# Language adapter with residual and layer norm on one core: the beginning ordered anew, a constant lag of the second product, and the inverse deviation as a power on GpSimd

## What is computed

```python
w1 = W1[language_ids]; w2 = W2[language_ids]
h = jnp.einsum('bsh,bha->bsa', hidden_states, w1) + b1[language_ids][:, None, :]
h = jax.nn.relu(h)
adapted = jnp.einsum('bsa,bah->bsh', h, w2) + b2[language_ids][:, None, :]
x = hidden_states + adapted
mean = jnp.mean(x, axis=-1, keepdims=True)
var = jnp.mean(jnp.square(x - mean), axis=-1, keepdims=True)
normed = (x - mean) * jax.lax.rsqrt(var + LN_EPS)
return hidden_states + normed * gamma[language_ids][:, None, :] + beta[language_ids][:, None, :]
```

## Time and profile before

| | |
|---|---|
| median of 3 runs | 348.10 us (347.31 to 348.62) |
| the profiled execution | 348.07 us |
| its span (first to last instruction) | 346.3 us |
| TensorE, busy | 305.1 us, 88% |
| VectorE, busy | 313.9 us, 91% |
| ScalarE, busy | 238.5 us, 69% |
| GpSimd, busy | 172.7 us, 50% |

### The profile page before, as it was taken

How to read it: one execution, slowest core, us unless ns; L and a number is a source line. 1 busy time by engine, 2 the same in 40 slices (tenths; PEclk the granted TensorE clock), 3 DMA queues, 4 the chain that set the end, 5 groups by cost and what they waited for, 6 DMA issues and landing times. The chain is left out here.

```text
span 346.3 us, 8118 instructions
## 1 busy us (share of the span) xinstructions
PE 305.1 (88%) x2196; PEld 273.1 (79%) x2196; DVE 313.9 (91%) x690; ACT 238.5 (69%) x599; POOL 172.7 (50%) x207
## 2 busy tenths in 40 slices
PE   2597799999799999979999998999999688988843
PEld 1186799998799999879999996999999577878731
DVE  4849789999999999999999999999999978788783
ACT  4348767788677777767777786777778565756532
POOL 1000066665655555565555566666666654635440
PEclk9999999999999999999999999999999999999996
DMA  7999805777776777677677777676777762231313
GB/s 218 314 413 398 313 13 173 243 245 244 241 243 232 231 238 241 224 252 236 235 237 235 232 235 250 234 237 236 242 245 242 242 223 101 107 120 65 122 61 121
DMA packets 41678, 75.63 MB, mean 218 GB/s; under 512 B 2250, under 2 KB 7401, under 8 KB 41509
## 3 DMA queue, kind: packets, MB, share of 16 engines
q1 hardware_dynamic: 41538, 74.98, 63.8%
q10 hardware_dynamic: 99, 0.14, 0.1%
HBM read 41.56 MB, written 33.55 MB: 217 GB/s over the span
## 5 line engine op out<-in xcount | busy, mean ns | idle before, releaser
L266 POOL TENSOR_TENSOR x_io<-x_io,beta_all 128x512 f32<-128x512 f32 x128 | 161.5, 1283 | 0.2 <-issue 0.2
L360 PE MATMUL ps_h<-w_all,x_T 128*128 x1024 | 143.8, 284 | 0.0
L360 PEld LDWEIGHTS ps_h<-w_all,x_T 128*128 128x128 f32 x1024 | 126.1, 194 | 1.5
L318 ACT ACTIVATE cut<-ps_y,row_sum 128x512 bf16<-128x512 f32 x128 | 87.9, 687 | 37.7 <-PE ps_y L382 37.7
L503 DVE SCALAR_TENSOR_TENSOR ps_y<-ps_y,mean,gamma_all 128x512 f32<-128x512 f32 x128 | 90.7, 752 | 14.1 <-ACT cut L318 13.6
L263 POOL TENSOR_TENSOR mean<-row_sum,over_h 128x2 f32<-128x2 f32 x64 | 12.6, 196 | 161.8 <-DVE ps_y L494 161.8
L516 DVE SCALAR_TENSOR_TENSOR x_io<-ps_y,rstd,x_io 128x512 f32<-128x512 f32 x128 | 90.2, 746 | 2.6 <-POOL x_io L266 0.3
L296 ACT COPY x_T<-ps_T 128x512 f32<-128x512 f32 x128 | 74.9, 588 | 21.0 <-PE ps_T L352 20.7
L494 DVE SCALAR_TENSOR_TENSOR ps_y<-x_io,b_all 128x512 f32<-128x512 f32 x128 | 87.4, 723 | 1.7 <-issue 1.7
L352 PE MATMUL ps_T<-identity,x_io 128*128 128x128 f32 x512 | 78.5, 277 | 6.2 <-DMA x_io<-in_x 6.2
L382 PE MATMUL ps_y<-w_high,h_high 128*128 x128 | 56.3, 439 | 15.2 <-DVE h_low L483 15.1
(11 more groups left out here) (43 smaller groups left out, 163.6 us busy)
## 6 DMA issues: line engine op xcount, KB each, us to landing
x_io<-in_x SPq DMA_DIRECT2D x64, 512.0 KB, 4.4
out<-x_io SPq DMA_DIRECT2D x63, 512.0 KB, 3.0
w_all<-in_L_cond_W SPq DMA_DIRECT2D x5, 512.0 KB, 8.1
x_io<-in_L_cond_W SPq DMA_DIRECT2D x5, 512.0 KB, 8.8
b_all<-in_L_cond_b SPq DMA_DIRECT2D x1, 2560.0 KB, 16.3
out<-x_io SPq DMA_DIRECT2D x2, 256.0 KB, 2.1
x_io<-in_L_cond_gamma ACTq DMA_DIRECT2D x1, 60.0 KB
x_io<-in_L_cond_beta ACTq DMA_DIRECT2D x1, 60.0 KB
```

What stands on the lines that cost most here:

```text
L266: nc.gpsimd.tensor_tensor(x_slot(t), x_slot(t), of_lang(beta_all, langs[b]), ALU.add)\
L318: nc.scalar.activation(squares[:, t % 2, :], ps_y[t % Y_BANKS][:, :], ACT.Square, scale=-float(H), bias=stat(row_sum, t), accum_out=stat(s ...
L360: last = nc.tensor.matmul(part, x_T[:, t % 4, c, :], w1_all[:, bass.ds(lang, 1), c, :].rearrange("p o a -> p (o a)"), start=False, stop=(c ...
```

## The change

**Order.** `FIRST` is 4 and the catch-ups are gone: steps 4 to 63 each have one second product, four pairs behind the first, and the last four pairs' second products follow step 63. h has six buffers in place of seven. In TensorE's step, `turn_h(p - 1)` now stands behind the first transpose of x and ahead of the first product, so that h is turned one step later than it was. ScalarE's step is: copy of x, rounding of h of the step before, copy of x, copy of h, then the squares.

**Beginning.** All 20 spreads stand ahead of step 0, over six banks (the four `ps_y`, `ps_h` and `ps_hT`); ScalarE copies gamma and the odd rows of beta, VectorE the even rows of beta. TensorE waits for all copies ahead of step 0. gamma's load is issued by SyncE ahead of x; ScalarE's table load comes ahead of its two DMAs. ScalarE's high halves of W2 stand ahead of the steps 0, 1, 2 and (two chunks) 3, each with its wait for the mean.

**Inverse.** VectorE's reciprocal is gone. GpSimd raises the deviation to the power -1, of pair n - 1, between the mean of pair n and its two additions of beta.

```diff
-H_PAIRS = 7
-FIRST = 5
-CATCH_UP = (12, 25, 38, 51)
+H_PAIRS = 6
+FIRST = 4
...
+    SPREAD_BANKS = Y_BANKS + 2
+    by_act = [n for n in range(2 * L) if n < L or n % 2 == 1]
+    by_dve = [n for n in range(2 * L) if n not in by_act]
...
             sp.dma_start(ids_raw[:, :], ids.rearrange("(a b) -> a b", a=1)).then_inc(s_ids, 16)
+            sp.dma_start(x_io[0:3 * L, 2 * ROWS_PAIR, :],
+                         gamma.unsqueeze(0).broadcast_to([3, L, H])).then_inc(s_gamma_rows, 16)
             load_x(0)
...
+            def invert_pair(n):
+                pool.wait_ge(std_ready, n + 1)
+                nc.gpsimd.tensor_tensor(stats(rstd, n), stats(std, n), minus_one[:, 0:2], ALU.pow).then_inc(rstd_ready, 1)
 
             def add_beta(n):
                 langs = langs_of(pool, n)
                 pool.wait_ge(seeded, 2 * n + 2)
                 pool.wait_ge(x_turned, 2 * n + 2)
                 nc.gpsimd.tensor_tensor(stats(mean, n), stats(row_sum, n), over_h[:, 0:2], ALU.mult).then_inc(mean_ready, 1)
+                if n > 0:
+                    invert_pair(n - 1)
                 for b in range(2):
                     t = 2 * n + b
                     nc.gpsimd.tensor_tensor(x_slot(t), x_slot(t), of_lang(beta_all, langs[b]), ALU.add)\
                         .then_inc(x_beta_ready, 1)
 
             pool.wait_ge(ids_ready, 1)
-            pool.wait_ge(over_h_ready, 2)
-            for p in range(PAIRS):
-                for n in second[p]:
-                    if n == 0:
-                        pool.wait_ge(spread_act, L)
-                        pool.wait_ge(spread_dve, L)
-                    add_beta(n)
-            for n in rest:
+            pool.wait_ge(over_h_ready, 3)
+            pool.wait_ge(spread_act, len(by_act))
+            pool.wait_ge(spread_dve, len(by_dve))
+            for n in range(PAIRS):
                 add_beta(n)
+            invert_pair(PAIRS - 1)
 
...
-            thrice = "(g l) h -> g l h"
-            act.dma_start(x_io[0:3 * L, 2 * ROWS_PAIR, :],
-                          gamma.unsqueeze(0).broadcast_to([3, L, H])).then_inc(s_gamma_rows, 16)
+            act.wait_ge(set_ready, 4)
+            nc.scalar.activation(table_load[:, :], eps[:, :], ACT.Sqrt, bias=eps[:, 0:1])
             act.dma_start(b1_rows[:, :],
                           b1.unsqueeze(0).broadcast_to([3, L, A])).then_inc(s_b1_rows, 16)
             act.dma_start(x_io[0:3 * L, 2 * ROWS_PAIR + 1, :],
                           beta.unsqueeze(0).broadcast_to([3, L, H])).then_inc(s_beta_rows, 16)
-            act.wait_ge(set_ready, 4)
-            nc.scalar.activation(table_load[:, :], eps[:, :], ACT.Sqrt, bias=eps[:, 0:1])
...
+            def step(p):
+
                 if p < PAIRS - 1:
                     copy_x(2 * p + 2)
+                if p > 0:
+                    high_h(p - 1)
+                if p < PAIRS - 1:
                     copy_x(2 * p + 3)
                 copy_h(p)
-                for n in second[p]:
-                    square_pair(n)
-                split_h(p)
-                for n in w2_after[p]:
-                    high_w2(n)
-            for n in rest:
+
+            copy_x(0)
+            copy_x(1)
+            for n in by_act:
+                act.wait_ge(spread, n + 1)
+                nc.scalar.copy(spread_to(n), spread_bank(n)).then_inc(spread_act, 1)
+            high_w2(0)
+            step(0)
+            high_w2(1)
+            step(1)
+            high_w2(2)
+            step(2)
+            high_w2(3)
+            high_w2(4)
+            step(3)
+            for p in range(FIRST, PAIRS):
+                step(p)
+                square_pair(p - FIRST)
+            high_h(PAIRS - 1)
+            for n in range(PAIRS - FIRST, PAIRS):
                 square_pair(n)
 
...
             langs = {0: langs_of(pe, 0)}
+            pe.wait_ge(b1_parts_ready, 1)
+            pe.wait_ge(spread_act, len(by_act))
+            pe.wait_ge(spread_dve, len(by_dve))
+            pe.wait_ge(s_w1, 16 * W_CHUNKS)
             for p in range(PAIRS):
-                for n in spread_before[p]:
-                    spread_row(n)
-                if p == 0:
-                    pe.wait_ge(b1_parts_ready, 1)
-                    pe.wait_ge(s_w1, 16 * W_CHUNKS)
                 for b in range(2):
                     pe.wait_ge(x_T_ready, 2 * p + b + 1)
                     if p < PAIRS - 1:
                         turn_x(2 * p + 2 + b)
+                    if b == 0 and p > 0:
+                        turn_h(p - 1)
                     first_product(2 * p + b, langs[p][b])
                 if p < PAIRS - 1:
                     langs[p + 1] = langs_of(pe, p + 1)
-                for n in second[p][:1]:
-                    if n == 0:
-                        pe.wait_ge(w2_low_ready, L)
+                if p == FIRST:
+                    pe.wait_ge(w2_low_ready, L)
+                if p >= FIRST:
+                    n = p - FIRST
                     for b in range(2):
                         second_product(2 * n + b, langs[n][b])
-                turn_h(p)
-                for n in second[p][1:]:
-                    for b in range(2):
-                        second_product(2 * n + b, langs[n][b])
-            for n in rest:
+            turn_h(PAIRS - 1)
+            for n in range(PAIRS - FIRST, PAIRS):
                 for b in range(2):
                     second_product(2 * n + b, langs[n][b])
 
...
-            copy_spreads(0)
-            dve.wait_ge(over_h_ready, 2)
+            for n in by_dve:
+                dve.wait_ge(spread, n + 1)
+                nc.vector.tensor_copy(spread_to(n), spread_bank(n)).then_inc(spread_dve, 1)
+            dve.wait_ge(over_h_ready, 3)
             mean_of_w2(0)
             mean_of_w2(1)
+            low_w2(0)
+            mean_of_w2(2)
+            low_w2(1)
+            mean_of_w2(3)
             low_h(0)
-            low_w2(0)
-            copy_spreads(1)
-            low_w2(1)
-            mean_of_w2(2)
-            mean_of_w2(3)
+            low_w2(2)
+            mean_of_w2(4)
+            low_w2(3)
             low_h(1)
-            low_w2(2)
-            copy_spreads(2)
-            mean_of_w2(4)
+            dve.wait_ge(ids_ready, 1)
+            langs = {n: langs_of(dve, n) for n in range(2)}
+            low_w2(4)
+            dve.wait_ge(s_b2, 16)
+            seed_pair(0, langs[0])
             low_h(2)
-            low_w2(3)
-            copy_spreads(3)
-            low_w2(4)
+            dve.wait_ge(spread_act, len(by_act))
+            dve.wait_ge(spread_dve, len(by_dve))
+            seed_pair(1, langs[1])
             low_h(3)
-            dve.wait_ge(ids_ready, 1)
-            dve.wait_ge(s_b2, 16)
-            dve.wait_ge(spread_act, L)
-            dve.wait_ge(spread_dve, L)
-            langs = {n: langs_of(dve, n) for n in range(2)}
-            seed_pair(0, langs[0])
-            low_h(FIRST - 1)
-            seed_pair(1, langs[1])
 
...
-                invert_pair(n)
                 finish_pair(n)
...
-            for p in range(PAIRS):
-                for n in second[p]:
-                    norm_and_seed(n, p if n == second[p][0] else None)
-            for n in rest:
-                norm_and_seed(n, None)
+            for n in range(PAIRS):
+                norm_and_seed(n, n + FIRST if n + FIRST < PAIRS else None)
```

More of the change, by code:

```diff
@@ L34, in build @@
     out_pairs = out.rearrange("(n b) s h -> s n b h", b=2)
[L38 to L53, removed]
+    SPREAD_BANKS = Y_BANKS + 2
+    by_act = [n for n in range(2 * L) if n < L or n % 2 == 1]
+    by_dve = [n for n in range(2 * L) if n not in by_act]
+    assert FIRST + 2 <= H_PAIRS
     with ExitStack() as ctx:
@@ L196, in of_lang, with spread_bank, pair_of @@
             return table[:, bass.ds(lang, 1), :].rearrange("p o h -> p (o h)")
+        spread_banks = ps_y + [ps_h, ps_hT]
+        assert len(spread_banks) == SPREAD_BANKS
+        def spread_bank(n):
+            return spread_banks[n % SPREAD_BANKS][:, :]
+        def pair_of(bank):
+            return bank[:, 0:2 * S]
         def flat(pair_tile):
@@ L370, in turn_h @@
                 for b in range(2):
-                    last = nc.tensor.transpose(ps_hT[:, b * S:(b + 1) * S], h_rows[:, p % 2, b, :], identity[:, :])
+                    last = nc.tensor.transpose(pair_of(ps_hT)[:, b * S:(b + 1) * S], h_rows[:, p % 2, b, :],
+                                               identity[:, :])
                 last.then_inc(h_turned, 1)
@@ L388, in _ @@
             turn_x(1)
[L389 to L393 removed]
+            pe.wait_ge(pick_ready, 1)
+            pe.wait_ge(parts_zero, 2)
+            pe.wait_ge(gamma_parts_ready, 1)
+            for n in range(2 * L):
                 if n == L:
                     pe.wait_ge(beta_parts_ready, 1)
[L396 to L397 removed]
+                gone = n - SPREAD_BANKS
+                if gone in by_act:
+                    pe.wait_ge(spread_act, by_act.index(gone) + 1)
```

(8 more changed lines are left out.)

36 lines of the change are left out of this document (6 added, 30 removed).

## The result

| | us |
|---|---|
| before, median of 8 runs | 347.98 (347.26 to 348.62) |
| after, median of 8 runs | 345.6 (344.91 to 346.83) |
| ratio after / before | 0.994, 95% interval 0.992 to 0.996 |
| forecast | 331 (326 to 344) |
| profiled execution of after, its span | 344.8, granted clock 0.974 (before 346.3, 0.991) |

The account below looks back on a forecast made before the run. It took TensorE as the early bound, then VectorE, then engines waiting in turn. Step 5 at 42.8 us plus 264.0 of steps, a tail to 326.4, 2.64 to the span's end and 1.8 outside gave 331 us (326 to 344).

Parts of the forecast that it names:

- Part 1, constant lag: Without catch-ups, TensorE paces at 4.49 us per step and the slow last twelve pairs go, returning about 11 us.
- period of 5.44: Distance in us between scalings after the last catch-up, pairs 52 to 63, engines waiting in turn; forecast to vanish.
- Part 2, the power: Inverse on GpSimd between mean and additions: VectorE's work falls to 4.23 us per pair, and the power costs nothing mid-kernel.
- The ring: GpSimd and VectorE, every pair: end of mean, P, additions, seeds; 4.14 + P us, the bound if P exceeds 0.35.
- P: Length of GpSimd's 128x2 power, without a row in the trace: taken as 0.30 us, ends 0.15 and 1.26.
- Each waits for the other to end: VectorE's seeds and GpSimd's additions of beta lock each other out for whole instructions, so a held seeding takes 1.25 us.
- Part 3, the beginning: Loads 0.7 us later, x pair 4 landing at 34.7, step 5 starting at 42.8; the start worth 4.7 us.
- The sum: Whole kernel: TensorE leaves the steps at 306.8 us, the last four pairs follow, span 329.0, plus 1.8 outside: 330.8.
- rival 1: GpSimd and VectorE: the ring becomes the bound mildly, P from 0.35 to 0.6; 340 us at P = 0.5; chance 0.25.
- rival 2: GpSimd and VectorE: the ring makes the kernel slower than before, P > 0.63; 358 us at P = 0.8; chance 0.14.
- Rival 4: VectorE's seeds aren't held by GpSimd's additions, the tail runs at VectorE's pace, P hardly counts: 329.5 us; chance 0.10.
- Rival 3: The new beginning gives nothing, step 5 starting at 47.4 us: 335.5 us in all; chance 0.06.

Follow-up runs that it names:

- the product: The changed kernel with a product in place of the power on GpSimd, same place and operands: 333.4 us, ratio 0.960.
- the two powers: The changed kernel with the power taken twice, the first time into a spare tile: 387.6 us, ratio 1.115.
- the seed with one SBUF operand: The changed kernel with the seed's second input taken from the PSUM bank in place of b2: 332.3 us, ratio 0.955.
- x pair 4 early: The changed kernel with the load of x pair 4 issued ahead of b2's: 344.3 us, ratio 0.992.
- the reciprocal kernel: The changed kernel with the inverse back on VectorE as a reciprocal, nothing else undone: 332.3 us, ratio 0.957.
- its like with the power ahead of the mean: The changed kernel with the power ahead of the mean and x pair 4's load ahead of b2's, no catch-ups: 330.8 us, ratio 0.954.
- the kernel with the lowest median: The changed kernel with the reciprocal back on VectorE and x pair 4's load ahead of b2's: 329.4 us, ratio 0.947.

## Why the prediction was wrong, point by point

**Part 1, constant lag: right.** TensorE paces at 4.49 us wherever nothing is held, with 755 matmuls in 100 us, and no period of 5.44 is left. The kernel with this part alone gains 12.6 us. The forecast had put about 11 us here.

**Part 2, the power: right mechanism, wrong size.** The ring (end of the mean, P, additions, seeds) and its place are borne out by the product, the two powers and the seed with one SBUF operand. The term that failed is P: I took 0.30 us because a 128x2 product on the same engine took 0.15 to 0.20, and the power takes 0.67. Both ends, 0.15 and 1.26, held it; my choice between them rested on the number of columns, as if the operation were nothing. It was a number without a row and with a threshold right beside it, and the expected cost as a mean over its bounds would have been far from zero. From there the step "TensorE paces the middle and the power costs nothing there" was wrong: the ring paces, at 4.69 us.

The ring's other terms were too long by 0.12 us: measured they add up to 4.02, not 4.14, which moves the threshold from 0.35 to 0.47. The recorded formula with P = 0.67 gives a round of 4.81 and, by 61 (P - 0.35), a span near 349; measured are 4.69 and 344.8. The 0.12 lie in the hold. A seed takes 0.61 us to its accumulator's reading (152.97 to 153.58 above). In after's round the held seed ends at 157.78, so by that length it was running from 157.17 on, 0.13 us before the recorded end of the additions at 157.30. "Each waits for the other to end" overstated the hold by that much.

The three kernels without the power's cost (reciprocal, product, seed with one SBUF operand) take 332.3 to 333.4 us, where the forecast had 331 with a power that costs nothing. So the rest of the sum was short by 1 to 2 us only.

**Part 3, the beginning: the loads right, 2 us missed.** x pair 4 landed at 34.13 (forecast 34.7). From there I let step 3 take 3.1 us; it took 5.97, at a granted clock of 0.50 up to 38 us. These 2.9 us were put at nothing: the forecast had the wait for x, but not the lower clock behind it, where eight matmuls take 2.02 and 1.94 us in place of 1.11 and four transposes 1.09 and 1.06 in place of 0.60. Step 4 took 4.74 us where I had 5.0. Step 5 came at 44.84, not at 42.8. VectorE's halves of W2 were ready by 34.8, earlier than the 36.8 of the forecast, and TensorE shows no wait for them. That "x pair 4 early" gave a step 5 at 42.21, near the 42.5 written for it, is luck: TensorE waited for h_low in step 3 and ran at the lower clock after it, and neither was in the sum. Also, the starts were worth less than they read: the reciprocal kernel has step 5 at 43.53, the kernel with the lag alone has the like point, with pair 0's second product behind it, at 47.27, 3.7 us apart; the spans of these two executions are 3.3 apart and the medians 2.5.

**The sum.** Forecast span 329.0, measured 344.8. Step 5: +2.0. From there to the end of the seeds of pair 63: 278.4 us forecast, 336.49 - 44.84 = 291.65 measured, +13.3 (61 rounds at 0.20 more are 12.2, the first round of 5.20 us another 0.7). The tail behind these seeds: 7.8 forecast, 8.3 measured, +0.5. Together 15.8, the whole of it.

**The rivals.** Rivals 1 and 2 were the same ring with a longer P, and it came out at their border: P = 0.67 is beyond rival 1's 0.6 and, by rival 2's P > 0.63, should have been slower than before. It wasn't, since the ring was 0.12 us shorter than its formula. Rival 4, seeds not held, is refuted by 0.95 us per seed and by the experiment that frees them. Rival 3 didn't come: the beginning gives something.

**In sums against before:** constant lag -12.6, order and beginning -2.5, power in that place +12.7; together -2.4.

## What to carry to other kernels

An operation moved to another engine has to be given the length of that operation on that engine; where the trace has no row for it and a threshold lies within its bounds, that one number is to be measured first, and the forecast should stand on the side where most of its bounds lie. Ahead of a long instruction that locks another engine out, count every step by what it shifts: here 0.47 us were free and each 0.1 us beyond cost about 6 us over 61 rounds. And before work is taken from an engine, see that this engine paces the kernel once the rest of the change is in: after the constant lag TensorE did, and VectorE's saved reciprocal was worth nothing.

## What was unexpected of the hardware

- A GpSimd power on 128x2 takes 0.70 us (0.67 to the next start), a product of the same shape 0.19 (0.14 to the next start).
- GpSimd's small instruction can be the one that stretches: a power that starts at 231.22, beside seeds at 231.26 and 231.86, shows 1.27 us in place of 0.70, and the seeds keep their 0.69 and 0.73.
- After a wait of 3.72 us in the beginning the granted clock read 0.50 from 34 to 38 us, and eight matmuls took 2.02 us. Other waits were not always followed by it: behind one of 2.52 us for h_low, eight matmuls took 2.02 us in the kernel with x pair 4 early (step 5 at 42.21), and 1.11 us in its like with the power ahead of the mean (step 5 at 40.79). What decides it the runs don't show.
- The mean granted clock differs between executions of one kernel: 0.963 in the one of 331.77 us of the kernel with the lowest median, 0.976 and 0.983 in its two of 328.7 us. They are 3 us apart, as much as the early load is worth, so one profiled execution of each kernel doesn't settle a difference of that size.
